# Gathers of segment ends at the close of a graph kernel's two convolutions, behind a wait for TensorE's last turn

## The reference

```python
def _egnn_conv(x, src, dst, edge_attr, W_msg, W_edge, W_root, b):
    msg = x[src] @ W_msg + edge_attr @ W_edge
    agg = jax.ops.segment_max(msg, dst, num_segments=x.shape[0])
    agg = jnp.where(jnp.isneginf(agg), 0.0, agg)
    return agg + x @ W_root + b
```

## Time and profile before

| what | value |
|---|---|
| median of 3 runs | 2313.93 us (2310.94 to 2314.37) |
| span of the profiled execution | 2309.6 us |
| TensorE busy | 2029.6 us (88%) |
| VectorE busy | 1235.0 us (53%) |
| ScalarE busy | 672.4 us (29%) |
| GpSimd busy | 763.4 us (33%) |
| gathers of messages, L1417 | 572, 1018 ns each |
| gathers of segment ends, L1633 | 50, 987 ns each |
| first convolution | to 777.96 us |
| second convolution | to 1324.75 us |

### The profile page before, as it was taken

How to read it: one execution, slowest core, us unless ns; L and a number is a source line. 1 busy time by engine, 2 the same in 40 slices (tenths; PEclk the granted TensorE clock), 3 DMA queues, 4 the chain that set the end, 5 groups by cost and what they waited for, 6 DMA issues and landing times. The chain is left out here.

```text
span 2309.6 us, 57334 instructions
## 1 busy us (share of the span) xinstructions
PE 2029.6 (88%) x23524; PEld 1918.6 (83%) x23524; DVE 1235.0 (53%) x3485; ACT 672.4 (29%) x1939; POOL 763.4 (33%) x762
## 2 busy tenths in 40 slices
PE   4599588888888668888888699999999999999998
PEld 3499487787777557787777699999999999999988
DVE  8946366666665336665666474444444444444635
ACT  6824112222221202222222133333333333333434
POOL 2566366655566256666656510000000000000000
PEclk9999799999999779999999899999999999999999
DMA  3055345555554435555555410000000000000000
GB/s 75 1 167 143 90 115 131 134 134 130 132 132 125 115 76 135 133 135 136 131 127 134 122 31 2 2 2 2 2 2 2 2 2 2 1 2 2 2 2 23
DMA packets 153147, 163.58 MB, mean 71 GB/s; under 512 B 43697, under 2 KB 141612, under 8 KB 152885
## 3 DMA queue, kind: packets, MB, share of 16 engines
q1 hardware_dynamic: 100493, 83.89, 14.1%
q0 software_dynamic: 20464, 32.18, 7.7%
q10 hardware_dynamic: 31928, 43.84, 5.3%
HBM read 100.90 MB, written 58.89 MB: 69 GB/s over the span
## 5 line engine op out<-in xcount | busy, mean ns | idle before, releaser
L1467 PE MATMUL c_taken<-rows,conv_hot 125*128 125x192 f16 x6500 | 646.6, 253 | 130.7 <-issue 113.4
L1417 POOL DMA_INDIRECT conv_rows<-messages,idx_all x572 | 582.2, 1018 | 418.2 <-issue 118.6
L1467 PEld LDWEIGHTS c_taken<-rows,conv_hot 125*128 125x128 f16 x6500 | 553.6, 101 | 188.7 <-issue 163.1
L1534 DVE TENSOR_SCALAR conv_hot<-head_offset_srcs 125x640 f16<-125x640 f16 x1300 | 344.9, 327 | 262.6 <-PE c_taken L1467 110.4
L1720 PE MATMUL l_ps<-rows,counts 125*128 125x192 f16 x5625 | 466.2, 246 | 1.9 <-DVE rows L1824 1.9
L1720 PEld LDWEIGHTS l_ps<-rows,counts 125*128 125x128 f16 x5625 | 464.0, 98 | 2.4 <-DVE rows L1824 2.4
L1720 PE MATMUL l_ps<-conv_rows,counts 125*128 125x192 f16 x5000 | 414.0, 246 | 0.8 <-DVE conv_rows L1865 0.8
L1720 PEld LDWEIGHTS l_ps<-conv_rows,counts 125*128 125x128 f16 x5000 | 412.6, 98 | 1.0 <-DVE conv_rows L1865 1.0
L1544 DVE TENSOR_TENSOR_SCAN c_scanned<-c_mask,c_scanned,c_msg 96x512 f32<-96x512 bf16 x208 | 264.6, 1272 | 175.6 <-DMA c_need<-deg 85.8
L1856 DVE SCALAR_TENSOR_TENSOR l_uf<-l_ps,l_cf,l_wide 125x96 f32<-125x96 f32 x400 | 127.1, 318 | 317.5 <-ACT l_wide L1791 317.5
L1597 ACT ACTIVATE c_back<-c_tr 128x384 f32<-128x384 f32 x208 | 102.3, 492 | 542.3 <-PE c_tr L1494 222.9
(11 more groups left out here) (297 smaller groups left out, 1770.9 us busy)
## 6 DMA issues: line engine op xcount, KB each, us to landing
running_max<-c_back ACTq DMA_DIRECT2D x208, 192.0 KB
c_attr<-attr_halves SPq DMA_DIRECT2D x412, 64.0 KB
c_mask<-segment_mask SPq DMA_DIRECT2D x206, 96.0 KB
conv_rows<-messages,idx_all POOLq DMA_INDIRECT x572
head_srcs<-sources SPq DMA_DIRECT2D x50, 160.0 KB
l0a_raw<-in_ea_t SPq DMA_DIRECT2D x50, 132.8 KB, 2.4
attr_halves<-l0a_hi SPq DMA_DIRECT2D x50, 66.4 KB, 2.0
attr_halves<-l0a_lo SPq DMA_DIRECT2D x50, 66.4 KB, 2.1
```

Source lines behind the costliest of these rows:

```text
L1417: pool.indirect_dma_start(out=gat[:, i % 2, j, :], out_offset=None, in_=c["y_d"], in_offset=bass.IndirectOffsetOnAxis(ap=idx_all[:, i * IT ...
L1467: return pe.matmul(acc[:, (NB * i + j // 2) % ACCS, j % 2 * (2 * F):(j % 2 + 1) * (2 * F)], hot[:, slot + k, j * ET:(j + 1) * ET], y[:, t, :],
L1534: last = v.tensor_scalar(hot[:, SLOTS[h % len(SLOTS)] + k, :], off[:, :], float(t * P - SRC_MID), None, ALU.is_equal)
```

## The change

Ahead of the second run (k = 1) GpSimd waits until `s_tr` stands at 108, that is, until TensorE has turned back the last group. The gathers themselves, their number, order and indices stay as they are.

```diff
@@ -1424,6 +1424,8 @@
                     pool.wait_ge(s_none, 17)
                 pool.sem_inc(s_gate, 1)
                 for k in range(2):
+                    if k == 1:
+                        pool.wait_ge(s_tr, N_IT * GT + GT)
                     for g, tiles in enumerate(by_dma):
                         early = [k * FROM_POOL + j for j in tiles if k * FROM_POOL + j < EARLY]
                         if early:
```

## The result

The changed kernel takes 2325.99 us (median of 6 runs, 2315.62 to 2332.46) against 2311.27 of the kernel before, measured again beside it (6 runs, 2297.42 to 2314.37): a ratio of 1.0063, 95% interval 1.0043 to 1.0084. It is slower by 10 to 19 us, where +1.3 was forecast. The profiled execution has a span of 2322.5 us, 12.9 more than that of before.

The account below looks back on a forecast made before the run. It took TensorE's last result, through ScalarE's copy and store, to set each convolution's end. The terms -20.0 + 17.8 + 3.0 + 0.5 gave +1.3 us, 2315.2 us on the median; range 2306 to 2326.

Parts of the forecast that it names:

- Term 1: Ends of both convolutions: with no gathers beside the last groups, TensorE's last turn comes 9.8 and 10.2 us sooner, -20.0 us.
- the crawl is not the gathers': Ends of both convolutions: last turns stay at 776.5 and 1323.4, all costs are added, +21.3 us, 2335; chance 0.13.
- Term 2: Barrier ending each convolution: waits until GpSimd hands over eleven gathers, start 10.3 us after last turn, not 1.4; +17.8 us.
- the barrier waits for the gathers: Barriers ending both convolutions: GpSimd arrives only behind the gathers, start 15.5 us after last turn, +8.2 us, 2322; chance 0.17.
- the slower rival: Same as "the barrier waits for the gathers": GpSimd's arrival at the two barriers, +8.2 us, 2322; chance 0.17.
- the low bound: Hand-over at each barrier: at the first run's pace, the next block starts 8.4 us after the last turn, not 10.3.
- Term 3: Blocks after each convolution: gathers running into them delay TensorE's first turn, +3.0 us, and loads after convolution 2, +0.5.
- TensorE only keeps warm: Block after convolution 2: VectorE leads, so only +0.5 us for root and state loads beside the gathers, 0 to 2.
- the sign against this term: Block after convolution 1: ScalarE's first copy at the old 7.3 us into it, or over 12, would show Term 3 wrong.

Follow-up runs that it names:

- The two changed profiles: The changed kernel as first profiled (2325.99 us against 2311.27), and the same kernel run again among the experiments (2049.66 us against 2035.96, ratio 1.0054).
- the kernel before again: The kernel before, nothing changed, run once more among the experiments for its own trace: a single run of 2048.18 us.

## Why the prediction was right or wrong

**Term 1, the last turn sooner: right in the first profile.** Last scans were foreseen at 764.8 and 1311.3. In convolution 1 it starts at 763.49; measured from the 97th scan TensorE is empty 11.6 and 10.7 us sooner, where 9.8 and 10.2 were forecast. The 1318.03 of convolution 2 is 7.3 us late only because everything ahead of it is (1293.68 against 1286.41). The rival "the crawl is not the gathers'" has fallen for that profile: with the second run moved away, the last two scans start 2.1 and 1.9 us apart instead of 5.8 and 8.6. Where TensorE runs at the faster pace the tails are the same with or without these gathers, and the term is zero.

**Term 2, the hand-over: the size right, the mechanism half.** The start 10.3 us behind the last turn was forecast; it is 9.7 and 9.9 us behind the drain's end, +8.2 and +8.5 where +8.9 was forecast, with gathers still starting. The rival "the barrier waits for the gathers" (15.5) fell. But I had argued from how far the queue may run ahead of the work, and had weighed, for the slower rival, a slow middle batch in the earlier trace rows as the sign of a queue nearly full. The two changed profiles hand over eleven gathers in the same 9.5 us with seven of them started in one and three in the other. It is a price of the issuing itself, whatever the engine behind does: 0.5 us a gather, 0.95 in the second run's middle batch, and 0.75 for each load with its marks. The forecast came close because it took its steps from that same second run of before, middle batch included; the low bound, which gave the middle batch the pace of the first run, did not hold. Why that batch takes 3.8 us stays open.

**Term 3, what runs into the next block: mis-sized, and here the prediction failed.** +3.0 and +0.5 were forecast, +10.2 and +7.8 measured. I counted gathers under way and put TensorE's first turn 0.8 us behind their end, 9.6 us in; it came at 14.5, 4.7 behind their end at 785.1. What I overlooked stands in the kernel's text: 80 and 240 idle matmuls ahead of the first useful one. A TensorE that is held has to work through these first. It stops some 44 matmuls into the block, resumes 2 us behind the last gather, and still has 29 and 193 of them to do, 3 and 13 us. For convolution 2 "TensorE only keeps warm" was the wrong reading: before, the 240 ended at 1340.3 (1324.79 + 15.54), 1.3 us ahead of the rows; a hold of 7 us had no more cover than that.
ScalarE's first copy came 15.7 us into the block, outside the old 7.3 and over the 12 that I had named as the sign against this term:

```profile
790.95 0.58 ACT L1121 ACTIVATE c2w_xt<-c2w_pt 96x500 f32<-96x500 f32 x1 [24.77 <-PE c2w_pt L1075]
```

Of the 10.2 us 7.9 lie ahead of the first turn. The other 2.3 come behind it, and their cause is not shown: among the experiments this stretch differs by as much between traces with nothing held. TensorE's granted clock may have a part in it; over the next 25 us it is 0.69 of full speed, against 0.86 over the 25 us that lie as far into that block before; both are means of stretches that lie partly at 1.2 and partly at 2.4 GHz.

```profile
787.30:812.30 25.00, 21.32 (x117) 18.63 (x114) 12.14 (x35) 8.35 (x21) 0.00 (x0) 0.69 0.29 78
```

```profile
790.00:815.00 25.00, 19.83 (x147) 17.46 (x147) 14.40 (x47) 6.33 (x16) 5.07 (x6) 0.86 0.51 131
```

(Columns: stretch, its length, busy time and instructions of PE, PEld, DVE, ACT and POOL, granted clock, DMA share, GB/s; first the changed kernel, then before.)

**The sum.** -22.3 + 16.7 + 18.0 = +12.4 in place of -20.0 + 17.8 + 3.5 = +1.3. The time lies at the very end of the range, which reaches so far for the rival that fell: that the range holds is luck. At the faster pace a similar total comes from other parts. Term 1 is 0 and the two barriers cost 15.1; the stretch from the first block's start to the next scan is 2.6 us shorter than in the kernel before again (41.7 against 44.4); +11 by the ratio and +13.7 by the medians remain. The change is slower there too, by term 2 alone.

**What stays open.** Why TensorE issues slowly beside long runs of gathers in one set of executions and not on the three chips of the experiments. That the chip makes the difference is not shown, since the record does not say which chip the first set ran on. That the idle matmuls are held by the gathers is read from one profile of the changed kernel. Against gathers alone speak the forty-odd matmuls that pass beside them, and SP's loads in the same stretch are a rival; no run could take either away at that pace.

## What to carry over

A wait that takes work off one engine's last stretch must be charged for everything the waiting engine still has to issue ahead of the next barrier, batch by batch, even if no one waits for the gathers to finish. When a stall is moved, look at what is queued first on the stalled engine at the new place: filler written to keep it warm becomes the critical path. And a gain that consists of ending a stall is worth only what the stall is in the executions that one cares for.

## What was not expected of the hardware

The kernel before took 2311 us in one set of runs and 2035 to 2039 in others, with the same instructions. TensorE's "issue" gaps in one group of matmuls come to 121 us in the changed kernel's first profile and to under 1 in its second. In the first case TensorE, beside a run of gathers, issued matmuls that wait for nothing 0.7 to 2.1 us apart (starts from 779.7 to 786.7), where 0.1 us is its pace. And GpSimd's queue took 0.5 us for a gather handed over, or 0.95 in one batch, the same whether none or seven of the eleven had been taken up by its engine, and all eleven could wait.
